# The late scores of a token attention in pairs of images instead of four images at once

## The reference, cut to what matters

```
def _L1_attn_ref(inputs):                       # inputs: (8, 256, 32), layer-normed tokens
    scores = jnp.einsum('bqd,bkd->bqk', inputs, inputs)
    weights = jax.nn.softmax(scores, axis=-1)
    return jnp.einsum('bqk,bkd->bqd', weights, inputs)

t = _to_tokens(x)
t = t + _L1_attn_ref(_ln_t(t))
t = t + _L1_ffn_ref(_ln_t(t), ...)
```

## Time and profile before

| what | value |
|---|---|
| median of 3 runs | 58.74 us (58.6 to 60.38) |
| the profiled execution, its own time | 58.65 us |
| its span | 56.5 us |
| mean granted TensorE clock | 0.999 |
| TensorE busy | 48.0 us, 85% of the span |
| VectorE busy | 38.7 us, 68% |
| ScalarE busy | 29.3 us, 52% |
| GpSimd busy | 20.2 us, 36% |

### The profile page before, as it was taken

The page is one execution under the profiler, slowest core; times in us unless marked ns, Lnnn a source line. Parts: engine busy times, 40 slices in busy tenths (PEclk is TensorE's granted clock), DMA queues, the critical chain, the costliest instruction groups (busy, mean ns, idle before and its releaser), DMA issues.

```text
span 56.5 us, 1445 instructions
## 1 busy us (share of the span) xinstructions
PE 48.0 (85%) x568; PEld 38.6 (68%) x568; DVE 38.7 (68%) x102; ACT 29.3 (52%) x68; POOL 20.2 (36%) x48
## 2 busy tenths in 40 slices
PE   3996997799699888999989947979999998979910
PEld 3994795687378776889867925655788585968600
DVE  2459399881849999959998475658368866685440
ACT  0813032696999396004865465297964839801000
POOL 6116389857678889960071040300000000000000
PEclk9999999999999999999999999999999999999999
DMA  0699941110000000000000000000000000000013
GB/s 0 158 194 274 240 158 46 59 46 22 0 0 0 0 0 12 6 0 0 0 0 0 0 0 6 0 0 12 0 0 0 0 0 0 12 0 0 0 49 137
DMA packets 3926, 2.02 MB, mean 36 GB/s; under 512 B 2640, under 2 KB 3792, under 8 KB 3920
## 3 DMA queue, kind: packets, MB, share of 16 engines
q1 hardware_dynamic: 1424, 1.37, 8.8%
q10 hardware_dynamic: 2496, 0.57, 4.7%
HBM read 1.68 MB, written 0.26 MB: 34 GB/s over the span
## 4 chain that ended last, share of the span: by engine, by line
PE 44%; DVE 19%; POOL 15%; ACT 7%; issue 5%; DMA 5%; DVEq 0%; ACTq 0%; POOLq 0%
DMA x_sb<-x_rows 5%; PE ps L711 4%; PE ps L792 4%; PE ps L917 3%; PE ps L858 3%; PE ps L900 3%; PE ps L804 3%; DVE taps L1100 3%; PE ps L922 2%; POOL w_smp L504 2%; ACT e_tok L654 2%; POOL d_prob L412 2%; PE ps L721 2%; DVE off L1102 2%; PE ps L747 2%
## 5 line engine op out<-in xcount | busy, mean ns | idle before, releaser
L711 PE MATMUL ps<-zeros 128*128 128x128 bf16 x128 | 10.8, 246 | 1.0 <-DVE zeros L1081 1.0
L711 PEld LDWEIGHTS ps<-zeros 128*128 128x128 bf16 x128 | 9.5, 113 | 1.5 <-DVE zeros L1081 1.0
L538 ACT ACT_TABLE_LOAD x4 | 5.1, 1283 | 1.7 <-PEq L1326 1.7
L654 ACT ACTIVATE e_tok<-ps,cst 128x512 f32<-128x512 f32 (+1 forms) x6 | 4.5, 828 | 1.5 <-PE ps L900 1.5
L1131 DVE COPY_PREDICATED ps<-over,ps 128x608 f32<-128x608 uint32 (+1 forms) x4 | 3.1, 776 | 0.7 <-PE ps L764 0.7
L453 POOL TENSOR_TENSOR wblk<-wts,cst 128x256 f32<-128x256 f32 x4 | 2.5, 625 | 2.4 <-DMA wts<-weights 2.4
L764 PE MATMUL ps<-rpe_blk,minus_hat_rel 128*32 128x168 f32 x64 | 2.8, 316 | 0.5 <-DVE minus_hat_rel L1127 0.5
L764 PEld LDWEIGHTS ps<-rpe_blk,minus_hat_rel 128*32 128x32 f32 x64 | 2.0, 141 | 1.3 <-issue 0.9
L527 POOL TENSOR_TENSOR x_tok<-ln_c 128x256 f32<-128x256 f32 x2 | 1.2, 617 | 4.7 <-ACT ln_c L639 4.7
L917 PE MATMUL ps<-e_tok,t 128*32 128x128 f32 (+1 forms) x48 | 2.8, 310 | 0.0
L900 PE MATMUL ps<-t_t 32*128 32x256 f32 x32 | 2.3, 398 | 0.4 <-ACT e_tok L654 0.4
(11 more groups left out here) (184 smaller groups left out, 126.8 us busy)
## 6 DMA issues: line engine op xcount, KB each, us to landing
w_sb<-weight ACTq DMA_DIRECT2D x1, 256.0 KB, 6.3
w_sb<-weight SPq DMA_DIRECT2D x1, 256.0 KB, 4.9
x_nat<-x_rows SPq DMA_DIRECT2D x8, 32.0 KB
wts<-weights SPq DMA_DIRECT2D x1, 192.5 KB, 3.9
cst<-shape_consts SPq DMA_DIRECT2D x1, 192.0 KB, 3.5
cst<-shape_consts SPq DMA_DIRECT2D x1, 130.0 KB, 4.8
x_sb<-x_rows SPq DMA_DIRECT2D x1, 128.0 KB, 2.7
x_sb<-x_rows ACTq DMA_DIRECT2D x1, 128.0 KB, 2.8
```

What stands on the lines that cost most here:

```text
L538: nc.scalar.add_instruction(mybir.InstLoadActFuncSet(name=nc.get_next_instruction_name(), act_func_set_id=functions, ins=[], outs=[]))
L654: return nc.scalar.activation(dst, scores, ACT.Exp, bias=const("bound"))
L711: mm(bank(n_bank, P), zeros[:, :], zeros[:, :], start=True, stop=True)
```

## The change

Nothing is computed otherwise, and there are as many instructions on each engine as before, in the same sizes. What changes is which images go together.

- Late scores: first all of images 4 and 5 (both key halves) into banks 2 and 3, behind a wait for the first exponent alone; then all of images 6 and 7 into banks 4 and 5, behind a wait for the second. Each pair raises `scores_done`.
- Late exponents: the large instruction takes all of images 4 and 5; the two small ones take images 6 and 7, one query half each.
- Early products: images 0 and 1, and then, behind their own wait for the third exponent, 2 and 3.
- Late sums and products: all of images 4 and 5 in both query halves, and then, for each query half behind a wait, those of images 6 and 7.

```diff
-        late_ps = ps[:, 1024:3072].rearrange("p (b h q) -> p b h q", b=B4, h=NHALF)
+        late_ps = [ps[:, 512 * a:512 * a + 1024].rearrange("p (b h q) -> p b h q", b=2, h=NHALF) for a, _ in first_banks]
...
             act.wait_ge(scores_done, 4)
-            exponent(e_tok[:, B4:, 0], late_ps[:, :, 0]).then_inc(exp_ready, 1)
+            exponent(e_tok[:, B4:B4 + 2], late_ps[0]).then_inc(exp_ready, 1)
+            act.wait_ge(scores_done, 5)
             for q in range(NHALF):
                 queries = slice(P * q, P * q + P)
-                exponent(e_tok[:, B4:, 1, queries], late_ps[:, :, 1, queries]).then_inc(exp_ready, 1)
+                exponent(e_tok[:, B4 + 2:, :, queries], late_ps[1][:, :, :, queries]).then_inc(exp_ready, 1)
...
+            def score_late(n):
+
+                pe.wait_ge(exp_ready, n + 1)
+                for h in range(NHALF):
+                    for b in range(2):
+                        last = score(late_ps[n][:, b, h], B4 + 2 * n + b, h, start=(h == 0))
+                return last
+
             for h in range(NHALF):
                 pe.wait_ge(x_tok_ready, h + 1)
                 last = turn_half(conv_ps, x_tok, h)
             last.then_inc(conv_done, 1)
 
+            score_late(0).then_inc(scores_done, 1)
+            score_late(1).then_inc(scores_done, 1)
+
             pe.wait_ge(ones_set, 1)
             pe.wait_ge(c_copied, NT)
-            pe.wait_ge(exp_ready, NHALF)
-            for h in range(NHALF):
-                for b in range(B4, B):
-                    last = score(late_ps[:, b - B4, h], b, h, start=(h == 0))
-            last.then_inc(scores_done, 1)
-
-            pe.wait_ge(exp_ready, NHALF + 1)
-            for h in range(NHALF):
-                for b in range(B4):
-                    last = attend(early_ot_ps, b, h, slice(0, M), start=(h == 0), stop=(h == 1))
+            for n in range(2):
+                pe.wait_ge(exp_ready, NHALF + n)
+                for h in range(NHALF):
+                    for b in range(2 * n, 2 * n + 2):
+                        last = attend(early_ot_ps, b, h, slice(0, M), start=(h == 0), stop=(h == 1))
             last.then_inc(ot_done, 1)
...
             pe.wait_ge(exp_ready, NHALF + 2)
+            def add_up_late(n, q):
+
+                for h in range(NHALF):
+                    for b in range(B4 + 2 * n, B4 + 2 * n + 2):
+                        last = add_up(late_sums_ps[:, q], b, e_tok[:, b, h, P * q:P * q + P], start=(h == 0), stop=(h == 1))
+                return last
+
+            def attend_late(n, q):
+
+                for h in range(NHALF):
+                    for b in range(B4 + 2 * n, B4 + 2 * n + 2):
+                        last = attend(late_ot_ps[q], b, h, slice(P * q, P * q + P), start=(q == 1 and h == 0), stop=(h == 1))
+                return last
+
             for q in range(NHALF):
-                queries = slice(P * q, P * q + P)
-                for b in range(B4, B):
-                    add_up(late_sums_ps[:, q], b, e_tok[:, b, 0, queries], start=True, stop=False)
-                for b in range(B4, B):
-                    attend(late_ot_ps[q], b, 0, queries, start=(q == 1), stop=False)
+                add_up_late(0, q)
+                attend_late(0, q)
             for q in range(NHALF):
-                queries = slice(P * q, P * q + P)
                 pe.wait_ge(exp_ready, NHALF + 2 + q + 1)
-                for b in range(B4, B):
-                    last = add_up(late_sums_ps[:, q], b, e_tok[:, b, 1, queries], start=False, stop=True)
-                last.then_inc(sums_done, 1)
-                for b in range(B4, B):
-                    last = attend(late_ot_ps[q], b, 1, queries, start=False, stop=True)
-                last.then_inc(ot_done, 1)
+                add_up_late(1, q).then_inc(sums_done, 1)
+                attend_late(1, q).then_inc(ot_done, 1)
```

## The result

The changed kernel takes 59.78 us (median of 6 runs, 59.47 to 60.09), the one before 58.88 (6 runs). The ratio is 1.018, with a 95% interval of 1.012 to 1.024. Timed again with the last experiments it was 1.0125 (1.006 to 1.019). So it is slower by 1.3 to 1.8%, some 0.7 to 1.0 us: clearly more than nothing, and not clearly 2%. 59.7 us had been forecast.

What follows compares the result with a forecast made beforehand. TensorE was taken to bound the kernel, with only two array strips working at a time for pairs. Sum: 0 + 0 - 0.07 (already in the 1.24) + 1.24 - 0.20 = 1.04; 58.65 + 1.04 = 59.7 us, range 58.6 to 60.9.

Steps and rivals of the forecast that it cites:

- Late scores: no gain on TensorE: Images 4 and 5 start 0.4 us earlier, 6 and 7 as before; the scores' end stays at 38.80.
- Late exponents: the idle 0.34 us goes and is worth nothing by itself: ScalarE's wait before the late exponents vanishes, but TensorE is late next, so no time is won.
- Early products and sums: nothing lost, and 0.07 us gained: New waits don't hold; strips 0 and 1 are through at 40.12, so the late stage starts there against 40.19.
- the fear that images 2 and 3 might start one or two passes late: Early products: this pair might start one or two passes of 0.22 us late; costed at nothing.
- the 0.07 of the forecast: Earlier start of the late sums and products, 40.12 against 40.19.
- Late sums and products: four passes of overlap, +1.24 us: TensorE starts the second pair four passes before the first ends, at 41.43; stage ends at 43.17 against 41.93.
- one that was shown and sixteen: TensorE's reach past waiting passes in a strip: one seen in the trace, up to 16 needed here.
- the deep reach: Rival: TensorE reaches far past the pair, late stage ends at 42.17, time 58.7 or 58.5; half way or further, 0.23.
- two ends: Late stage ends at 43.60 without taking up the second pair early, or 42.17 as soon as its exponent allows.
- Give-back of 0.20 us: TensorE's wait for ScalarE's square, before the squares at 43.01, disappears and returns 0.20 us.
- the 1.04 of the forecast: TensorE goes on with the squares behind the late stage at 44.05 against 43.01, 1.04 us later.

Runs made afterwards that it cites:

- the last experiments: Kernel before with late work by query halves, one gate-logit matmul between the squares and three behind: 58.27 us, ratio 0.991; the unedited changed kernel was timed on the same chip.

## Why the prediction was right

**Late scores: no gain on TensorE.** Nearly right: the early products behind them start at 38.82, less 0.13, against 38.80, so there was a gain of 0.11 us.

**Late exponents: the idle 0.34 us goes and is worth nothing by itself.** Right: six exponents in one piece of 4.43 us, and the time went up all the same.

**Early products and sums: nothing lost, and 0.07 us gained.** Right, and the fear that images 2 and 3 might start one or two passes late was empty. Within 38.82 to 38.86 all four strips have begun:

```profile
38.82 0.44 PE L918 MATMUL ps<-e_tok,t 128*32 128x256 f32 x4
```

A strip has four passes there, so three wait: just within the reach. The late stage starts at 40.14, less 0.13, which is 0.18 us earlier than before: the 0.11 of the scores and the 0.07 of the forecast.

**Late sums and products: four passes of overlap, +1.24 us.** This term carried the forecast. Four passes had been chosen between one that was shown and sixteen; in the trace four overlap (one that starts, three that wait). The stage had been put at 41.43 for the second pair and 43.17 for the end. With the 0.13 taken off they are 41.34 and 43.11, and the stage before really ended at 41.98 instead of 41.93, since the strips don't start at quite the same time. So the term was 1.13. The forecast's line of the sum writes -0.07 beside it, though that is in the 1.24 already, as its bracket says; and where it lets the deep reach wait for the fourth exponent, at 40.28, it means the fifth. Neither changes a result. The choice had been between two ends with little to tell them apart; that it fell on the right number is in part luck.

**Give-back of 0.20 us.** Right. TensorE's squares of the first late half come at 44.05; less 0.13 this is 0.91 later than 43.01, for the 1.04 of the forecast. In the profiled times the move is 59.65 against 58.65, 1.00, with the 0.13 in it, so that the profiled time meets the 59.7 more closely than the working does.

## What to carry to other kernels

In these runs, small matmuls in strips of the array were only side by side where the program brought the strips in turn: blocks of up to four passes (two float32 matmuls) a strip cost nothing, blocks of eight and sixteen made the stage longer. Other types than float32 weren't tried. A regrouping that lets one engine start earlier, but makes runs of the same strip longer, is to be priced by those runs, pass by pass. If data arrives in pairs, alternate the pairs in short blocks, or cut the work so that every group has all strips and the part that is needed first (here a query half) is finished first. The two came out alike, at 0.996 and 0.997 of the time before, and at 0.993 and 0.9935 with the logits moved.

## What the runs showed of the hardware that had not been expected

- TensorE goes past three waiting passes of a strip to the next strip; a fourth holds up what is behind it. Blocks of 4, 8 and 16 passes in two strips gave stages of 1.98, 2.30 and 3.10 us (0.2 of the 1.98 is the wait for an exponent), blocks of 16 in one strip 5.77. It is counted for each strip: two strips with three each, or one, give the same start. That was measured with passes of 128 columns. For 256 columns the early products show only that three waiting passes hold nothing up. What in the engine sets the number isn't shown.
- The granted clock stayed at 1.00, its level of 2.4 GHz, through the stage with half of the array idle, as this table by stretch shows (length, busy time and count of PE, PEld, DVE, ACT and POOL, clock, DMA):

```profile
40.14:41.45 1.31, 1.31 (x28) 1.30 (x24) 0.85 (x2) 0.80 (x3) 0.00 (x0) 1.00 0.00 0
41.45:41.90 0.45, 0.45 (x20) 0.45 (x18) 0.00 (x0) 0.45 (x2) 0.00 (x0) 1.00 0.00 0
41.90:43.24 1.34, 1.34 (x32) 1.24 (x24) 0.56 (x3) 0.17 (x1) 0.00 (x0) 1.00 0.00 0
```

The table also shows that busy time doesn't tell two strips from four: PE is busy all the time in the first and last stretch (two strips) and in the middle one (four). The passes tell: some 28 in 1.31 us against 20 in 0.45.
